# Second attention of a two-layer kernel: elu's negative part on ScalarE, and a new order of elu, roots and routed rows

## The reference, cut to what matters

```python
def _L1_attn_ref(x, norm_w, Wq, Wk, Wv, Wo, Wu):
    ...
    q, k, v = (proj(Wq), proj(Wk), proj(Wv))
    pq = jax.nn.elu(q) + 1.0
    pk = jax.nn.elu(k) + 1.0
    ...
    A = jnp.einsum('bnchk,bndhk->bnhcd', pqc, pkc) * tri
    intra = jnp.einsum('bnhcd,bndhv->bnchv', A, vc)
    ...
    attn_w = jax.nn.softmax(jnp.concatenate([sc_cached, sc_cur], axis=-1), axis=-1)
    gates_cached = attn_w[..., :N]
    gate_current = attn_w[..., N:]
    h_retrieved = jnp.einsum('btn,bthk,bnhkv->bthv', gates_cached, pq, boundary_states).reshape(B, T, D)
    return gate_current * x_out + retrieval_scale * h_retrieved

def _L1_ffn_ref(x, gate_w, gate_b, w1, b1, w2, b2):
    probs = jax.nn.softmax(xt @ gate_w + gate_b, axis=-1)
    _, idx = jax.lax.top_k(probs, TOP_K)
    ...
```

## Time and profile before

| | before |
|---|---|
| median of 3 runs | 619.88 us |
| profiled execution | 613.83 us |
| its span | 612.1 us |
| mean granted clock of PE | 0.855 |
| PE busy | 495.4 us (81%) |
| DVE busy | 380.1 us (62%) |
| ACT busy | 291.9 us (48%) |
| POOL busy | 288.2 us (47%) |

### The profile page before, as it was taken

How to read it: one execution, slowest core, us unless ns; L and a number is a source line. 1 busy time by engine, 2 the same in 40 slices (tenths; PEclk the granted TensorE clock), 3 DMA queues, 4 the chain that set the end, 5 groups by cost and what they waited for, 6 DMA issues and landing times. The chain is left out here.

```text
span 612.1 us, 14071 instructions
## 1 busy us (share of the span) xinstructions
PE 495.4 (81%) x4416; PEld 396.7 (65%) x4416; DVE 380.1 (62%) x1175; ACT 291.9 (48%) x824; POOL 288.2 (47%) x375
## 2 busy tenths in 40 slices
PE   5889999998996499997056989799789872999990
PEld 3655666665654499997055767576577552999990
DVE  4677689795756354644787567747865764543333
ACT  2233554645352366667235466536444320766650
POOL 3524445448277535655420433324462666356650
PEclk9978899997867599999567799988896765999995
DMA  7999000001000221321999200000000002213316
GB/s 238 307 305 359 3 1 2 2 1 37 2 22 33 72 63 57 93 79 36 327 307 336 115 2 2 2 1 2 10 28 3 19 28 67 72 49 91 90 35 214
DMA packets 28374, 53.71 MB, mean 88 GB/s; under 512 B 4816, under 2 KB 24208, under 8 KB 27248
## 3 DMA queue, kind: packets, MB, share of 16 engines
q1 hardware_dynamic: 23216, 42.17, 21.6%
q0 software_dynamic: 4544, 9.45, 4.6%
q10 hardware_dynamic: 544, 1.20, 0.6%
HBM read 42.32 MB, written 29.81 MB: 118 GB/s over the span
## 5 line engine op out<-in xcount | busy, mean ns | idle before, releaser
L1618 ACT ACTIVATE probs<-ps,w1s 128x128 f32<-128x128 f32 x312 | 89.1, 369 | 46.3 <-PE ps L2038 46.2
L776 POOL DMA_INDIRECT ybuf<-yt,xg x78 | 75.9, 974 | 64.1 <-DVE yt L1164 55.8
L2038 PE MATMUL ps<-xgT,w1s 128*128 128x128 f32 x624 | 86.0, 282 | 1.4 <-ACT xgT L1609 0.8
L2046 PE MATMUL ps<-w,probs 128*128 x624 | 82.2, 276 | 0.0
L2038 PEld LDWEIGHTS ps<-xgT,w1s 128*128 128x128 f32 x624 | 78.8, 198 | 2.7 <-issue 1.2
L721 POOL DMA_INDIRECT xbuf<-rsc,sloti x64 | 63.3, 989 | 28.8 <-DVE yt L1164 11.4
L811 POOL TENSOR_SCALAR_AFFINE_SELECT probs<-probs 128x512 f32<-128x512 f32 x64 | 39.2, 637 | 78.6 <-ACT probs L1719 78.5
L2046 PEld LDWEIGHTS ps<-w,probs 128*128 128x128 f32 x624 | 75.7, 192 | 0.0
L894 DVE TENSOR_REDUCE negm<-ps 128x2 f32<-128x512 f32 (+1 forms) x96 | 60.3, 685 | 24.2 <-PE ps L1871 19.5
L1532 ACT ACTIVATE probs<-ps 128x512 f32<-128x512 f32 x96 | 51.2, 601 | 36.7 <-PE ps L1894 36.4
L666 POOL TENSOR_SCALAR_AFFINE_SELECT probs<-probs 128x512 f32<-128x512 f32 x64 | 39.2, 637 | 59.1 <-ACT probs L1532 59.1
(11 more groups left out here) (275 smaller groups left out, 1088.1 us busy)
## 6 DMA issues: line engine op xcount, KB each, us to landing
xbuf<-in_c_pads SPq DMA_DIRECT2D x16, 1122.0 KB, 18.8
xg<-xbuf SPq DMA_DIRECT2D x78, 66.0 KB, 1.9
w<-in_w SPq DMA_DIRECT2D x2, 2064.0 KB, 35.5
w<-in_w SPq DMA_DIRECT2D x2, 2048.0 KB, 35.9
w<-ybuf SPq DMA_DIRECT2D x8, 512.0 KB, 5.5
ybuf<-yt,xg POOLq DMA_INDIRECT x78, 2.3
probs<-in_c_sel ACTq DMA_DIRECT2D x2, 512.0 KB, 5.1
bias<-in_b SPq DMA_DIRECT2D x2, 512.0 KB, 31.6
```

Source lines behind the costliest of these rows:

```text
L776: pool.indirect_dma_start(out=ybuf[l][:, :], out_offset=bass.IndirectOffsetOnAxis(ap=xg[n % AHEAD][:, D:D + 1].bitcast(I32), axis=0), in_= ...
L1618: ins = act.activation(hidT[n % 3][:, c * P:(c + 1) * P], ps[:, q, c * P:(c + 1) * P], ACT.Gelu if l == 0 else ACT.Relu, bias=w[:, FF + c: ...
L2038: mm = pe.matmul(ps[:, n % 2, c * P:(c + 1) * P], w[:, c * P:(c + 1) * P], xgT[n % 2][:], start=True, stop=True)
L2046: mm = pe.matmul(ps[:, 6 + n % 2, 0:D], hidT[n % 3][:, c * P:(c + 1) * P], w2[:, ds(e * FF + c * D, D)], start=(c == 0), stop=(c == FC - 1))
```

## The change

Four things, all in the second attention:

1. min(x, 0) is no longer made by DVE. ACT makes relu(-x) from the same PSUM bank, and the exponential takes scale -1 of it. Both stand in step s = 3 of ACT, ahead of `exp_scores`.
2. DVE does `elu` and `round_elu` ahead of `gate_chunks`; `own_scores` stays behind it.
3. POOL does `roots` behind `rest_of1` and `mask1`.
4. For groups 0 and 1, DVE does `give_slots` behind `own_scores` and `norm_rows` one step later, and ACT does `copy_rows` behind `copy_scores`. Groups 2 and up keep their places.

```diff
@@ POOL, steps of the second attention
-                    if group(1, 4 * c + s) >= 0:
-                        roots((1, group(1, 4 * c + s)))
                     if s == 0 and inside(c + 1):
                         rest_of1(c + 1)
                     if inside(c):
                         mask1(4 * c + s)
+                    if group(1, 4 * c + s) >= 0:
+                        roots((1, group(1, 4 * c + s)))
@@ DVE
-            def elu_min(b):
-
-                wait(dve, "proj", b, 1)
-                wait(dve, "elu_exp", b, 0)
-                signal(dve.tensor_scalar(rot[0][:], bank1("proj", b), 0.0, None, ALU.min), "elu_min")
-
@@
                     q = due(1, u, "slots")
-                    if q >= 0:
+                    if q >= COUNTED:
                         give_slots(1, q, bank1("rank", q))
@@
-                    if s == 2 and inside(c + 2):
-                        elu_min(c + 2)
+                    if s == 3 and inside(c + 2):
+                        elu(c + 2)
+                        round_elu(c + 2)
                     if s == 3 and inside(c + 1):
                         gate_chunks(c + 1)
                     if s == 3 and inside(c + 2):
-                        elu(c + 2)
-                        round_elu(c + 2)
                         own_scores(c + 2)
+                    if 0 <= q < COUNTED:
+                        give_slots(1, q, bank1("rank", q))
                     combine_rest(c, s)
...
-                    if group(1, u) >= 0:
+                    if group(1, u) >= COUNTED:
                         norm_rows(1, group(1, u))
+                    if 0 <= group(1, u - 1) < COUNTED:
+                        norm_rows(1, group(1, u - 1))
@@ ACT
             def elu_exp(b):
+                wait(act, "proj", b, 1)
+                wait(act, "elu_exp", b, 0)
+                signal(act.activation(rot[0][:], bank1("proj", b), ACT.Relu, scale=-1.0), "elu_min")
                 wait(act, "elu_min", b, 1)
                 wait(act, "elu", b, 0)
-                signal(act.activation(rot[1][:], rot[0][:], ACT.Exp), "elu_exp")
+                signal(act.activation(rot[1][:], rot[0][:], ACT.Exp, scale=-1.0), "elu_exp")
@@
-                    if q >= 0:
+                    if q >= COUNTED:
                         copy_rows(1, q, [bank1("rT", q, n) for n in range(rT_banks(q))])
                     if s == 2 and inside(c + 2):
                         copy_xT1(c + 2)
+                    if s == 3 and inside(c + 2):
+                        elu_exp(c + 2)
                     if s == 3 and inside(c + 1):
                         exp_scores(c + 1)
-                    if s == 3 and inside(c + 2):
-                        elu_exp(c + 2)
                     if inside(c):
                         copy_scores(4 * c + s)
+                    if 0 <= q < COUNTED:
+                        copy_rows(1, q, [bank1("rT", q, n) for n in range(rT_banks(q))])
```

## The result

| | before | changed |
|---|---|---|
| median, 20 runs each | 620.0 us | 620.19 us |
| profiled execution | 613.83 us | 620.42 us |
| its span | 612.1 us | 618.7 us |
| PE busy | 495.4 us | 492.0 us |
| DVE busy | 380.1 us | 380.0 us |

The ratio to the kernel before is 1.0071, with a 95% interval of 1.0041 to 1.0102: inside 2% of no change, and if anything slower. The forecast was 607 us, the range 600 to 618. The ratios of this document leave out executions in which the chip was in a slower state (the second profile of gates first comes from one), so they need not be the quotient of the medians.

What follows compares the result with a forecast made beforehand. No engine is full; PE's list is the longest, held up by gaps between sequences, mostly waits for `elu` and masks. Net gains of 9.0 us plus 4 of clock, 13.0 off 619.88, gave 607 us, range 600 to 618.

Steps and rivals of the forecast that it cites:

- The base: Whole kernel: sum made on the profiled trace (613.83 us), taken off the median of three runs, 619.88 us.
- the gaps named as gaps behind `elu`: PE's idle gaps between sequences of the second attention, put down to `elu`: 1.15, 1.29, 1.02, 1.72, 1.08 and 0.8 us.
- Part 1: Minimum on ACT: DVE loses 0.68 us per sequence, ACT gains a 0.6 relu covered by idle time, no table load.
- Part 2: `elu` ahead of the gates: starts 1.73 us earlier in sequence 4, covering PE's gap; `gate_chunks` about 1 us late.
- the second rival: The gap changes its owner: PE waits ahead of `look_states` for the bank `own_scores` holds; 614 us, chance 0.22.
- The terms 0.95, 0.8, 1.1, 0.8 and 0.9: Gains in us from PE's closed gaps in sequences 2, 3, 4, 5 and 7, with `elu` ahead of the gates.
- Part 3: Roots behind masks on POOL: group 0's 2.88 us PE gap goes, 2.9 saved; group 2 loses 0.9.
- Part 4: Routed rows: `norm_rows` free within DVE's 2.75 us slack; late `give_slots` leaves sequence 6 only 0.55 of its 1.72 gain.
- The clock: PE at 1.2 GHz behind gaps, windows 390 to 470 us: 4 us regained, ends 0 and 10.6.
- The third and fourth rivals: Routing takes the path, bare `norm_rows` and late slots: 625 us, chance 0.10; tables switched: 627 us or more, 0.01.

Runs made afterwards that it cites:

- gates first: The changed kernel with `gate_chunks` back ahead of `elu`: 595.82 us against 606.36 for the kernel before, ratio 0.9818; on chip D 0.9822.
- the minimum alone: The kernel before with only the minimum moved to ACT as relu and exp, plus the later copy of rows: ratio 0.9965 to the kernel before.
- roots and rows alone: The kernel before with POOL's roots behind rest and masks and `norm_rows` a step later, minimum still on DVE, slots early: ratio 0.9874.

## Why the prediction was wrong

**The base.** It stood: 211.1 and 210.7 us for the stage before. One reading was loose: of the gaps named as gaps behind `elu`, the 1.29 of sequence 2 ends by its row on POOL's masks, as does the 0.98 of sequence 6.

**Part 1** was right in its costs. The relu takes 0.60 on ACT (0.6 forecast), its wait is in ACT's idle time, and no table load stands in the stage. What DVE shed, 0.68 per sequence, it spent again in the gates.

**Part 2 failed**, and it is the step on which the result turned: "What becomes late is `gate_chunks`, by about 1 us". The working costed the gates at their 1.21 us wherever they stand. It asked what they make late, not what runs beside them in their new place. They began about 0.6 later behind `retrieve`, met the masks and the rest there, and grew by 1.9 to 2.05 us in five sequences. The sequel, PE held by the bank of `own_scores`, was the second rival, at 0.22 and 614 us. Its mechanism came, but for a cause that it didn't name, and the point against it, "PE reaches that bank about a microsecond after DVE lets go", held only for gates of 1.21: they were 2 us longer, and PE waited 1.15. How the changed kernel's lead over the one before ran, by the start of `elu` from the stage's start, beside that of gates first:

| sequence | 1 | 2 | 3 | 4 | 5 | 6 | 7 | end of stage |
|---|---|---|---|---|---|---|---|---|
| changed, us ahead | 3.1 | 3.3 | 1.8 | 1.7 | 5.9 | 3.3 | 1.3 | -2.0 |
| gates first, us ahead | 2.0 | 2.4 | 3.5 | 4.4 | 11.2 | 12.1 | 9.9 | 11.4 |

In the upper line about 1.2 us of each entry, the length of the gates, is only that `elu` stands ahead of them in its step. The jump at sequence 5 is part 3's: +4.2 above, +6.7 below. From there the upper line loses everything: from 5 to 6 in a stretch at 1.2 GHz (412.1 to 422.3), from 6 to 7 at the late slots, where the lower line loses 2.2 too, and then in the tail.

The terms 0.95, 0.8, 1.1, 0.8 and 0.9 were credited to `elu` ahead of the gates. Gates first shows that the minimum's move closes nearly all of these gaps without it: PE's wait for `elu` in sequence 4 is 0.20 there. That closing them is worth their sum in time is not shown: the minimum alone measured 0.35%, about 2 us.

**Part 3** was right in kind and too small in sum. Forecast were 2.9 for the gap, less 0.9, and 2.6 of clock behind it, 4.6 together; alone, the part brought 1.3% [0.6 to 2.0], some 8 us. At the place itself, between the first scores of sequences 3 and 4, the forecast was right: PE idles 2.9 less and is busy 2.6 less (1.8 against the other profile of the kernel before). The mis-sized term is the clock further on: in the whole stage PE was busy 6.1 us less, where 2.6 was taken for this place and 1.4 for all others. In the changed kernel this gain was used up: its stage has PE as busy as before, 166.8 against 166.6. For group 2 DVE waited 2.25 for the roots, more than the upper end of 1.7; what of it reached PE was not separated.

**Part 4** placed the work well and missed the price. POOL reached the rest and masks at 439.52 and 440.74 (440.5 and 441.8 forecast), but 8.8 us behind `elu` of the sequence instead of 6.1, and PE waited 3.51. The path is the one that the working followed, the slots behind `own_scores` on DVE, then the two scatters (1.04 and 0.96), then the rest, then the masks on POOL; what it had wrong is the distance to `elu`, on which PE's wait hangs. The stretched gates are not needed for it: with gates first, and gates of 1.19 there, PE waits 3.30 and 3.32 at the same place.

**The clock** was the second step that failed. Its term was a gain of 4 us, 0 at the least; in the middle of the stage the changed kernel lost by it. From the first scores of sequence 1 to those of sequence 5 PE does the same work in every kernel (781 or 782 matmuls):

| from sequence 1 to 5 | PE's time | busy | idle |
|---|---|---|---|
| before, two profiles | 82.5, 83.1 | 71.3, 71.9 | 11.2, 11.2 |
| changed, three profiles | 82.5, 82.8, 82.4 | 74.2, 74.4, 74.2 | 8.3, 8.4, 8.3 |
| roots and rows alone | 75.4 | 67.1 | 8.3 |
| gates first, two profiles | 73.5, 71.9 | 68.7, 67.1 | 4.8, 4.8 |

The changed kernel idles as long as the roots and rows alone: what the minimum and `elu` ahead of the gates took off PE's waits came back as waits for `own_scores`. And the 2.9 us that part 3 saved in idle time went into longer busy time, with a granted clock of 0.90 where the kernel before had 0.94 and the roots and rows alone had 1.00.

"Where the gap of 2.88 stood the stretch is the likeliest to go" held; with the roots alone it went. In the changed kernel it came back in other places: L2140 takes 1.10 at 393.43 and 2.06 at 415.94, the latter behind waits of 0.49 and 0.91. That a gap of about a microsecond alone does it is not shown: with the roots alone the clock held at 1.00 over a gap of 1.14. What in the order of `elu` and gates makes the clock fall stays open.

**The third and fourth rivals.** The routing didn't take the path by bare `norm_rows`; its term for the late slots (POOL idle 2 us more) did occur (2.44). No tables were switched.

What stays open: how the 13.4 us between the changed kernel and gates first divide over the whole stage. In the first pair of profiles 4.8 of it is PE busy longer and 8.6 is idle time, in the pair on chip D 8.7 and 3.8. What repeats is the middle of the stage, in the table above: 9 to 11 us, of them 3.5 idle and 5.5 to 7 longer busy at a lower clock.

## What to carry to other kernels

When an instruction is moved, read what the other engines do at its new place, and not only what waits for it: small VectorE instructions from SBUF lasted here as long as the GpSimd instruction that they fell beside (1.20 for 0.16), and those that read PSUM did not, so it is the latter that belong beside GpSimd's work. One stretched instance in the trace of before (0.48 and 0.56 where the others have 0.16 and 0.17) is worth more than the mean of its group. And after an edit that shortens a chain, try it alone before adding an order change meant to shorten the same chain: here the first had already closed the gap that the second was costed against.

## What the runs showed of the hardware

- A TensorTensor of 128x2 from SBUF on DVE took 0.16 us alone, 0.48 to 0.60 beside a mask (the two masks of a step take 1.22 together) and 1.17 to 1.20 beside the 1.27 us rest. A TensorScalar of 128x2, with one SBUF operand, was stretched as well: 0.17 to 0.56 and 1.21. The reciprocal of 128x2 never was (0.17), nor were the instructions of the stage that read PSUM (0.68 to 0.69 for 128x512, 0.41 to 0.42 for 128x256). POOL's rest stays the same (1.26 to 1.28).
- The cast of 128x512 from SBUF took 0.43 alone and 0.77 to 0.80 where it began beside a step's masks.
- Between chips the same two mixtures took 98 and 96 us or 102 and 101, so times from different chips are not to be compared.
- In the changed kernel PE was granted 1.2 GHz from 395.1 to 398.4, behind waits of 1.15 at 375.51 and at 393.43; with the roots and rows alone it kept 2.4 GHz behind waits of 0.80 and 1.14.
